# Swapped operands for the attention values and a fused post-norm step in a four-block cross-attention kernel

## The reference

```
L0: x += attn(ln(x)) W + b;  x += cross(ln(x), ctx) W + b;  x += gelu(ln(x) W1 + b1) W2 + b2     (causal self attention)
L1: x += cross(rms(x), ctx) W                                                                       (q and k rotated by rope)
L2: x = ln(x + attn(x) W + b);  x = ln(x + cross(x, ctx) W + b);  x = ln(x + gelu(..) W2 + b2)     (masks, norm after)
L3: x += attn(ln(x)) W + b;  x += cross(ln(x), ctx) W + b;  x += gelu(ln(x) W1 + b1) W2 + b2
attn: softmax(q k^T / sqrt(8)) v per head
```

## Time and profile before

| | |
|---|---|
| median of 3 runs | 2332.77 us (2331.26 to 2337.57) |
| the profiled execution, its own time | 2326.22 us |
| its span, first to last instruction | 2323.9 us |
| mean granted TensorE clock | 0.981 |
| busy: PE / PEld / DVE / ACT / POOL | 2108.6 / 1726.2 / 1829.7 / 1647.3 / 1384.1 us |
| units, time per unit | 448, about 5.2 us |

### The profile page before, as it was taken

The page is one execution under the profiler, slowest core; times in us unless marked ns, Lnnn a source line. Parts: engine busy times, 40 slices in busy tenths (PEclk is TensorE's granted clock), DMA queues, the critical chain, the costliest instruction groups (busy, mean ns, idle before and its releaser), DMA issues.

```text
span 2323.9 us, 100781 instructions
## 1 busy us (share of the span) xinstructions
PE 2108.6 (91%) x40685; PEld 1726.2 (74%) x40685; DVE 1829.7 (79%) x4657; ACT 1647.3 (71%) x3278; POOL 1384.1 (60%) x3557
## 2 busy tenths in 40 slices
PE   2789989899999998999999998989999999899987
PEld 2577867687888776777888787768788877677765
DVE  3589887787888887777888888778788889877764
ACT  0367756687887775777888775668788777577775
POOL 3355446886555444888555544688655544488843
PEclk6899999999999999999999999999999999999999
DMA  6355555454555555544555555544455545554432
GB/s 149 91 135 135 134 134 133 113 120 117 131 133 127 136 136 136 125 115 114 133 131 133 129 134 139 131 118 120 117 133 129 123 120 123 136 127 114 120 95 58
DMA packets 310571, 289.18 MB, mean 124 GB/s; under 512 B 50080, under 2 KB 251552, under 8 KB 310112
## 3 DMA queue, kind: packets, MB, share of 16 engines
q1 hardware_dynamic: 305120, 279.80, 48.9%
q10 hardware_dynamic: 4128, 1.65, 0.4%
q0 software_dynamic: 864, 1.28, 0.3%
HBM read 130.51 MB, written 34.60 MB: 71 GB/s over the span
## 4 chain that ended last, share of the span: by engine, by line
PE 48%; POOL 20%; SPq 10%; DVE 7%; ACT 6%; issue 5%; DMA 4%; DVEq 1%; POOLq 0%; ACTq 0%
PE ps_scores_t L837 7%; PE ps_scores L790 6%; PE ps_turn L891 6%; PE ps_turn L821 6%; SPq L531 6%; PE ps_wide L919 5%; PE ps_turn L896 3%; POOL x L645 2%; DVE row_max L1145 2%; PE ps_wide L916 2%; DMA k_slots<-k_dram 2%; PE ps_wide L866 2%; PE ps_wide L867 2%; PE ps_wide L873 2%; POOL post_rstd L603 2%
## 5 line engine op out<-in xcount | busy, mean ns | idle before, releaser
L1145 DVE TENSOR_REDUCE row_max<-ps_scores 128x16 f32<-128x1024 f32 x448 | 547.4, 1222 | 306.3 <-PE ps_scores L790 139.3
L1151 DVE TENSOR_TENSOR shifted<-ps_scores,row_max 128x512 f32<-128x512 f32 x896 | 598.7, 686 | 15.4
L731 ACT ACTIVATE probs<-ps_scores_t 128x512 f32<-128x512 f32 x896 | 486.3, 595 | 79.7 <-PE ps_scores_t L837 77.6
L721 ACT COPY pv_sb<-ps_turn 128x256 f32<-128x256 f32 x448 | 167.0, 373 | 361.5 <-PE ps_turn L821 357.1
L790 PE MATMUL ps_scores<-k_slots,qk_rows 32*64 32x256 f32 x7168 | 311.4, 403 | 49.7 <-DMA k_slots<-k_dram 43.5
L821 PEld LDWEIGHTS ps_turn<-probs,v_ones 128*32 128x32 f32 x14336 | 222.0, 110 | 151.7 <-ACT turned L702 75.9
L837 PE MATMUL ps_scores_t<-ident,shifted 64*128 64x64 f32 x7168 | 321.5, 230 | 11.4 <-DVE attn L1163 7.7
L837 PEld LDWEIGHTS ps_scores_t<-ident,shifted 64*128 64x128 f32 x7168 | 260.0, 140 | 54.9 <-ACT turned L702 9.3
L821 PE MATMUL ps_turn<-probs,v_ones 128*32 128x64 f32 x14336 | 294.7, 223 | 4.2 <-ACT turned L702 2.0
L702 ACT COPY turned<-ps_turn 128x256 f32<-128x256 f32 (+2 forms) x466 | 192.2, 412 | 125.5 <-PE ps_turn L954 111.1
L726 ACT ACT_TABLE_LOAD x190 | 243.8, 1283 | 3.3
(11 more groups left out here) (172 smaller groups left out, 4539.9 us busy)
## 6 DMA issues: line engine op xcount, KB each, us to landing
v_ones<-v_rows SPq DMA_DIRECT2D x1792, 64.0 KB, 2.3
k_slots<-k_dram SPq DMA_DIRECT2D x448, 256.0 KB, 3.3
k_dram<-qk_rows SPq DMA_DIRECT2D x448, 64.0 KB, 2.8
x_in<-in_x SPq DMA_DIRECT2D x64, 64.0 KB, 2.0
ctx_in<-in_ctx SPq DMA_DIRECT2D x64, 64.0 KB, 2.0
out<-x SPq DMA_DIRECT2D x64, 64.0 KB, 1.8
k_dram<-zeros SPq DMA_DIRECT2D x4, 256.0 KB, 6.0
w<-in_L_xattn_W SPq DMA_DIRECT2D x2, 256.0 KB, 6.4
```

Source lines behind the costliest of these rows:

```text
L731: nc.scalar.activation(probs[:, b, :, :], ps_scores_t[:, b, :] .rearrange("p (h t) -> p h t", t=LEN), ACT.Exp, scale=SCALE).then_inc(probs ...
L1145: v.tensor_reduce(row_max[:, :].rearrange("p (g n) -> p g n", n=SLOTS), ps_scores[:, :, 0:256].rearrange("p g (n k) -> p g n k", k=LEN), A ...
L1151: v.tensor_tensor(shifted[:, j % 2, u, :].rearrange("p (g n k) -> p g n k", n=SLOTS, k=LEN), ps_scores[:, 2 * u:2 * u + 2, 0:256].rearrang ...
```

## The change

Three things are changed.

1. `values` swaps its operands: probs becomes the weight (64 columns, tiles of 128 rows by 64 columns, two at a time) and v_ones moves (32 columns). The result has tokens on partitions at once, in ps_scores_t, so the ACT copy (L721), the transposes `pv_t` (L908) and their waits are removed.
2. The order and distance of the steps change. VALUES, TURN_OUT and OUT become 1, 2 and 3. On PE transposes follow the scores directly, project stands before mlp_down, and values come after turns and rope_v, ahead of mlp_up only. On DVE normalise opens the phase, ahead of maxima, and belongs to the values of the phase before; residual comes before mlp_residual and, where there is no down step, before both shifts. Transposes now always wait for the attn of the unit before.
3. A post norm's subtract and multiply become one DVE operation (`post_norm_scale`, one phase after the root), and its gain and shift stay on POOL, behind a wait for it, as the first steps after attention_bias. The POOL steps of a post norm are thus split over two phases.

```diff
-VALUES, TURN_OUT, OUT = 2, 3, 4
+VALUES, TURN_OUT, OUT = 1, 2, 3
...
 def post_norm_end(r, j, norm, g, scaled, ready):            # POOL
-    inverse_root(r, j, norm)
-    normalised(r, j, norm, x[:, s, :]).then_inc(norm.root.sem, 1)
-    pool.wait_ge(norm.root.sem, norm.root.at(r, j, 4))
+    pool.wait_ge(scaled.sem, scaled.at(r, j))
     pool.tensor_tensor(normed, normed, post_g, ALU.mult)
     pool.tensor_tensor(x, normed, post_b, ALU.add)
...
 def phase(r, j):                                            # POOL
     attention_bias(r, j + 1)
-    post_norm_end(r, down, ...)
-    post_norm_end(r, out, ...)
-    mlp_norm_end(r, out)
-    mlp_bias(r, out)
+    post_norm_end(r, down - 1, ...)
+    post_norm_end(r, out - 1, ...)
+    mlp_bias(r, out - 1)
+    inverse_root(r, down, mlp_post_norm)
+    inverse_root(r, out, post_norm)
+    mlp_norm_end(r, out)
     pre_norm_end(r, j + STATS)
...
-    copy_pv(r, j - VALUES)                                  # ACT, first in the phase
...
 def values(r, j):                                           # PE
-    for u in range(HALVES):
+    for n in range(HEADS // 2):
         for b in range(SEQS_OF_PAIR):
-            for h in range(4):
-                matmul(ps_turn[32 * h:32 * h + 32, u * P + 64 * b:u * P + 64 * b + 64],
-                       v_ones[:, f, b, 4 * u + h, :], probs[:, b, 4 * u + h, :])
+            matmul(ps_scores_t[64 * b:64 * b + 64, 0, n * V_COLUMNS:(n + 1) * V_COLUMNS],
+                   probs[:, b, n, :], v_ones[:, f, b, n, :])
 def transposes(r, j):                                       # PE
-    if exists(r, j - VALUES):
-        pe.wait_ge(attn_ready.sem, attn_ready.at(r, j - VALUES))
+    pe.wait_ge(attn_ready.sem, attn_ready.at(r, j - 1))
...
 def phase(r, j):                                            # PE
     scores(r, j)
+    transposes(r, j - 1)
     turned_free(r, j)
-    values(r, j - VALUES)
-    transposes(r, j - 1)
-    pv_taken(r, j - VALUES)
-    mlp_down(r, j - DOWN)
     project(r, j - OUT)
+    mlp_down(r, j - DOWN)
     qkv(r, j + QKV)
-    pv_t(r, j - VALUES)
     turns(r, j)
     rope_v(r, j + QKV)
+    values(r, j - VALUES)
     mlp_up(r, j - UP)
...
+def post_norm_scale(r, j, norm, scaled):                    # DVE
+    dve.wait_ge(norm.root.sem, norm.root.at(r, j, 2))
+    v.tensor_scalar(normed, x, mean_var[:, b, 0:1], rstd[:, b:b + 1],
+                    ALU.subtract, ALU.mult).then_inc(scaled.sem, 1)
...
 def phase(r, j):                                            # DVE
+    normalise(r, j - VALUES - 1)
     maxima(r, j)
-    shift(r, j, 0)
-    if late: shift(r, j, 1); mlp_residual(r, j - DOWN)
-    residual(r, j - OUT)
-    if not late: shift(r, j, 1)
+    if down: shift(r, j, 0)
+    residual(r, j - OUT)
+    if down: mlp_residual(r, j - DOWN)
+    else: shift(r, j, 0)
+    shift(r, j, 1)
+    post_norm_scale(r, below, ...)
+    post_norm_scale(r, out, ...)
     mlp_post_norm_begin(r, j - DOWN)
     post_norm_begin(r, j - OUT)
     rope_products(r, j + QKV)
-    normalise(r, j - VALUES)
     rope_sum(r, j + QKV)
...
```

More of the change, by code:

```diff
@@ L370, in of_round @@
             return dram[r, s]
-        PHASES = range(-STATS, UNITS + LAG * STREAMS + DOWN + 2)
+        PHASES = range(-STATS, UNITS + LAG * STREAMS + DOWN + 3)
         def rounds(phase):
@@ L817, in values @@
                     pe.wait_ge(probs_ready.sem, probs_ready.at(r, j))
-                    for u in range(HALVES):
+                    for n in range(HEADS // 2):
                         for b in range(SEQS_OF_PAIR):
-                            for h in range(4):
[L821 to L824, removed]
+                            ins = nc.tensor.matmul(ps_scores_t[64 * b:64 * b + 64, 0, n * V_COLUMNS:(n + 1) * V_COLUMNS],
+                                                   probs[:, b, n, :], v_ones[:, f, b, n, :], start=True, stop=True)
                     ins.then_inc(pv_ready.sem, 1)
                 def transposes(r, j):
-                    if exists(r, j - VALUES):
-                        pe.wait_ge(attn_ready.sem, attn_ready.at(r, j - VALUES))
+                    pe.wait_ge(attn_ready.sem, attn_ready.at(r, j - 1))
                     if exists(r, j + QKV) and layer_of(j + QKV) == L1_CROSS:
@@ L897, in project @@
                                      start=True, stop=True).then_inc(y_ready.sem, 1)
[L899 to L905, removed]
-                        pe.wait_ge(probs_ready.sem, probs_ready.at(r, j + VALUES - 1, 1))
-                    for u in range(HALVES):
-                        ins = nc.tensor.transpose(ps_scores_t[:, 0, u * P:(u + 1) * P], pv_sb[:, u, :],
-                                                  ident[:, :])
-                    ins.then_inc(pv_t_ready.sem, 1)
                 def mlp_up(r, j):
@@ L1201, in phase @@
                     rope = exists(r, j + QKV) and layer_of(j + QKV) == L1_CROSS
+                    if exists(r, j - VALUES - 1):
+                        normalise(r, j - VALUES - 1)
                     if exists(r, j):
                         maxima(r, j)
-                    late = has_mlp(r, j - DOWN)
-                    if exists(r, j):
+                    down = has_mlp(r, j - DOWN)
+                    if down and exists(r, j):
                         shift(r, j, 0)
-                        if late:
-                            shift(r, j, 1)
-                    if late:
-                        mlp_residual(r, j - DOWN)
                     if exists(r, j - OUT):
                         residual(r, j - OUT)
-                    if exists(r, j) and not late:
-                        shift(r, j, 1)
+                    if down:
+                        mlp_residual(r, j - DOWN)
+                    elif exists(r, j):
+                        shift(r, j, 0)
+                    if exists(r, j):
+                        shift(r, j, 1)
+                    below, out = j - DOWN - 1, j - OUT - 1
+                    if exists(r, below) and layer_of(below) in MLP_POST_NORM:
+                        post_norm_scale(r, below, mlp_post_norm, mlp_post_scaled)
+                    if exists(r, out) and layer_of(out) in POST_NORM:
+                        post_norm_scale(r, out, post_norm, post_scaled)
                     if has_mlp(r, j - DOWN):
```

51 lines of the change are left out of this document (25 added, 26 removed).

## The result

The changed kernel takes 2357.45 us in the median of 4 runs (2353.20 to 2363.18), the one before 2332.02 in its 4 runs beside it. The ratio is 1.0106 with an interval of 1.0077 to 1.0136: **25 us slower**, between 18 and 32. The profiled execution of the changed kernel took 2363.18 us, 37 more than that of before.

What follows compares the result with a forecast made beforehand. PE's own work was taken to bound most stages, POOL a few. PE work +137, waits removed -137 and new waits +50 gave +50 on 2332.8, so 2383 us; own range 2345 to 2430, 8-in-10 range 2300 to 2460.

Steps and rivals of the forecast that it cites:

- step 5 (a): PE's turns wait for DVE's residual, which shares ps_turn: about 0.1 us a phase, 448 times, +45 us.
- values, 448 times: On PE, values with swapped operands take 1.04 us instead of 0.58 per unit, 16 rounds instead of 8: +206 us.
- one more shape change, 192 times: On PE where mlp_up follows values: 0.10 us to drain full tiles plus 0.05 for the bf16 opener, +29 us.
- v_rows and rope_b: PE's waits on the ACT copy and rope_b, 118 waits, get covered by values standing last: -49 us.
- x from POOL, mlp_normed: PE's waits on these norm results go as post-norm subtract and multiply leave POOL: -47 us.
- k_slots: PE's wait on DMA shrinks through earlier qkv, an earlier rope sum and longer PE phases: -41 us.
- transposes for attn and shifted: PE's transposes wait for attn of the unit before where no mask or mlp_up intervenes: 146 x 0.15, +22 us.
- overlap with today's waits: Part of PE's new waits already stands in today's waits for x, so +67 us was taken as +50.
- Rival D: Weight loads and matmuls of values on PE add up, values take 1.46 us: 188 us more, 2571; chance 0.04.
- rival C: DVE becomes the bound, normalise, maxima and residual slip, PE stands at transposes and turns: +90 us, 2473; chance 0.12.
- B: Faster: nearly all PE stall in POOL-set and k_slots stages goes, new waits don't show: -36 us, 2297; chance 0.24.
- E: Whole kernel: costs and savings cancel, no change within 0.3%, 2333 us; chance 0.12.

Runs made afterwards that it cites:

- four-tile form: Changed kernel with each 64-column weight of values cut into two of 32 on four column tiles, 64 matmuls instead of 32: 2361.79 us, ratio 1.0110.
- values part alone: Changed kernel with the whole post norm put back on POOL, values, order and distances as changed: 2367.68 us, ratio 1.0142.
- norm part: Kernel before with only the post norms' subtract and multiply moved to the head of DVE's phase, one phase later: 2304.58 us, ratio 0.9880.
- doubled project: project issued twice, first result overwritten: on the changed kernel 2448.76 us; on the kernel before with only the post-norm change 2366.51 us.

## Where the prediction was right, and where it was wrong

The direction and the mechanism hold: PE's work grows, its waits shrink by less than that, the kernel is slower. The size does not: +50 was forecast, +37 came out between the two profiled executions, +25 between the medians, half of the forecast. The term that was most wrong is step 5 (a), PE's turns waiting for DVE's residual: +45 us were put down for it, and -7 were measured. The working was made against one execution and carried over to the median; as the two executions lie at opposite ends of their runs, 12 of the missing 25 us can't be charged to any step. The other 13 can be looked for, by the prediction's own rule (idle time as shown plus 0.165 us for each wait):

| step | forecast | measured |
|---|---|---|
| values, 448 times | +206 | +211 (1.055 against 0.585 us, start to start) |
| pv transposes | -98 | -98 |
| one more shape change, 192 times | +29 | +18 (0.095 each) |
| PE's work | **+137** | **+131** |
| v_rows and rope_b | -49 | -49, gone |
| x from POOL, mlp_normed | -47 | -47, gone |
| k_slots | -41 | -35 |
| pv_sb (17 waits) | 0 | -11, gone |
| turns for the residual | +45 | -7 |
| transposes for attn and shifted | +22 | +65 |
| overlap with today's waits | -17 | |
| PE's waits | **-87** | **-84** |
| not accounted for | | -10 |
| sum | **+50** | **+37** |

The sum of PE's waits, -84 against -87, is right by luck: the turns are 52 us too high, the transposes 43 too low, and the 17 us of overlap, for which the working gives no row, were not found. So the terms that failed most do not make up the 13 us. By the table the forecast had 6 us too much for PE's work and 3 too little for its waits, and 10 are in no row. Where those 10 lie stays open, but they are inside PE's own stream. Added up from start to start over both whole traces, values take 216 us more, scores and masks 51 more, qkv, project, mlp_down, mlp_up and the score transposes 23 more, and pv_t, turns and rope_v 254 less with the waits behind them: +37 in all. So single prices of the table are off, such as the 0.165 us for each wait; which of them is not shown.

**Values** came out at 1.055 us where 1.04 was forecast, from the loads of L762. Rival D falls: 64 moving columns left the 1.06 as it was. The rule from the Trainium skill's "TensorE: Matmul & The Clock Gate", Part 3, that the prediction set against the trace, is contradicted twice, here and in the four-tile form. The same skill's "TensorEngine Tiling (Array Packing)", Performance Considerations, by which a moving operand of 32 columns should rather be the stationary one on four column tiles, agrees: that is the form of the kernel before, with 0.585 us against 1.055 for the group, and the kernel with the values part alone is 33 us slower.

**The shape change** was mis-sized: 0.15 taken, 0.095 found. The drain into the values costs the 0.10 assumed (803.81 to 804.02), but the bf16 opener of mlp_up, for which half of 0.10 was taken, is no dearer after values than it was before: 0.226 us to the next group in both, in the median.

**The turns** are the step that failed most, step 5 (a), +45 against -7. The prediction set PE's arrival at 2.25 us after the scores' first matmul and the residual at 2.4, for every phase but those with a down step. That leaves out two things that delay PE there more than DVE. In a masked phase (scores at 1261.30) the residual ends at 2.4 and the turns start at 2.6. In the unmasked one at 805.07 the residual ends at 2.2, while the transposes had waited for attn in that same phase. A phase that has paid at the transposes need not pay again at the turns: two waits in series on one engine were priced as if each came alone. And the 47 waits on residuals that the kernel before already had (17.6 us) were left out of the count; 7 of 4.9 us are left, while start to start 148 phases show 0.08 us, 12 in all, that no wait shows.

**The transposes** failed the other way. The count was right, 146 units with neither a mask nor mlp_up behind the values, but each costs 0.32 us in the mean, 47 us, not 0.15. The 0.14 at 805 (0.76 against 0.62) is about the least that occurs, and 76 of the 146 units pay no more. In the other 70 DVE comes late: it is still at norm statistics, or in 20 of them at the rope sum, when the values are done, and the transposes start 0.90 to some 1.6 us after the scores. Over all 448 units PE ended the reciprocal's wait in only 125 (68.7 us). That is rival C's mechanism, at the transposes rather than at the turns, and of a third of its size (146 x 0.18 = 26 us against 90). Masks don't cover all of it either, 11 us in 184 units; the rest of the 65 lies in the filling and the emptying of the pipeline. Leaving out the division took 27 us off, so this wait is real.

**The filling of the pipeline** was not considered. Where a unit has nothing else on PE, transposes straight behind scores stand for shift: 15.8 us in 8 waits in the first stage, against 2.1 in one before. It is 65.4 us long instead of 55.4, once per launch, 10 of the 37.

**Waits that went** were right in kind and nearly in size, but not all by the cause given. They were taken as independent of the rest, and the two halves of the change measured apart show that they are not: with the post norms whole on POOL, PE's waits for x and mlp_normed are gone as well, covered by its longer phase. The norm part brings 8 us on top of the values and 28 alone.

**The clock** doesn't explain the rest. The mean granted clock was 0.981 in the one profile and 0.992 in the other, and the difference lies mostly in the start-up. From 20 to 57 us TensorE was granted 0.50 (1.2 GHz) before and 1.00 (2.4 GHz) after, but it is busy there for 7 of 37 us in both:

```profile
20.00:57.00 37.00, 6.78 (x27) 5.34 (x27) 12.32 (x74) 3.14 (x9) 4.85 (x13) 0.50 0.55 119
20.00:57.00 37.00, 7.24 (x35) 5.67 (x43) 12.10 (x72) 3.14 (x9) 4.87 (x13) 1.00 0.56 122
```

The first scores start at 57.56 and 56.54 us, so this cost some 1 us at most. From 57 to 113 us the clock was 0.80 and 0.83. The 33 runs of the kernel before that were timed beside the experiments say the same: the 9 with a mean clock of 0.985 or more took 2334.0 us in the mean, the 24 below 0.983 took 2334.2.

**The rivals.** B (faster, all stall gone) needed values at 0.95 us or less. The four-tile form is below that in 343 of 448 units and is still not faster, because k_slots and attn took the time back; so B's premise that the new waits don't show was wrong as well. C decides nowhere: in the stage at 81.2 us DVE is busy for 62.6, and its lateness costs the 26 us above, not 90. E is out, since the interval begins 18 us above no change. That PE's work is paid nearly in full, on which the forecast's side rests, is shown by the doubled project: 92% in the changed kernel, 61% in the one with the norm part alone.

## What to carry to other kernels

Swapping the operands of a small matmul is priced by rounds of tiles: count them before and after, and take for each the slower of load and moving side; here fewer instructions elsewhere did not pay for twice the rounds. Before moving work off an engine that sets a few stages, ask whether another part of the same change already covers those stages: two savings in one place don't add up. Where a step is moved next to its producer, look for the consumer that now follows it too closely, and don't charge one phase for two waits in series.

## What the runs showed of the hardware

- With float32 weights of 64 columns on two column tiles of 128 rows a round takes about 0.057 us ((1.055 - 0.08 - 0.12) / 15), half of the 0.112 of a 128-column load in the earlier trace rows; under it 32 or 64 moving columns cost the same (1.05 and 1.06 us for the group).
- The same work as 64 matmuls on four column tiles takes 0.69 us in the median instead of 1.05, with pauses of over 0.15 us in 42 of 448 units that no semaphore explains. Beside it the median landing of x_in went from 2.1 to 2.9 us and the instruction queue moved 7.05 MB instead of 5.21.
- Leaving full tiles costs 0.10 us in the pass before (0.21 for 0.11); coming back costs a bf16 matmul nothing that can be seen (0.226 us to the next group with and without).
